# Image network with early fusion, one core: TensorE's four layers of a half batch written out instead of looped

## The reference

```python
x = coords @ fc0_w + fc0_b                 # 3 -> 32 channels
for sw, cw, cb in four_layers:
    x1 = _spectral_conv(x, sw)             # rfft2, a mix of 20 x 20 modes, irfft2
    x2 = einsum('bchw,oc->bohw', x, cw) + cb
    x = _gelu(x1 + x2)
x = _gelu(x @ fc1_w + fc1_b)
return (x @ fc2_w + fc2_b)[..., 0]
```

## Time and profile before

| | |
|---|---|
| median of 3 runs | 4595.69 us (4594.42 to 4607.03) |
| profiled execution, its own time | 4594.02 us |
| its span, first to last instruction | 4592.3 us |
| TensorE busy | 3972.5 us, 87% of the span |
| VectorE, ScalarE, GpSimd busy | 2471.1, 549.6, 651.3 us |
| mean granted clock of TensorE | 0.761 of full speed |

### The profile page before, as it was taken

The page is one execution under the profiler, slowest core; times in us unless marked ns, Lnnn a source line. Parts: engine busy times, 40 slices in busy tenths (PEclk is TensorE's granted clock), DMA queues, the critical chain, the costliest instruction groups (busy, mean ns, idle before and its releaser), DMA issues. The chain is left out here.

```text
span 4592.3 us, 117705 instructions
## 1 busy us (share of the span) xinstructions
PE 3972.5 (87%) x48492; PEld 3374.7 (73%) x48492; DVE 2471.1 (54%) x8074; ACT 549.6 (12%) x1173; POOL 651.3 (14%) x1708
## 2 busy tenths in 40 slices
PE   6999999999999999697657677898999989988687
PEld 5887888768888887454335576788998989986544
DVE  4444544244444452223656888787686775662422
ACT  0101011210010102211211110101000010001011
POOL 1000000000000000000002423232231231222121
PEclk9999999999999999787755555555555555556589
DMA  1000000000000000100003110101000000013111
GB/s 35 15 16 2 15 2 15 2 5 15 1 15 16 1 1 2 24 0 4 8 12 85 29 36 28 31 28 31 24 22 30 21 30 18 19 32 87 20 36 28
DMA packets 189733, 96.94 MB, mean 21 GB/s; under 512 B 139462, under 2 KB 172534, under 8 KB 188631
## 3 DMA queue, kind: packets, MB, share of 16 engines
q1 hardware_dynamic: 183574, 84.19, 7.8%
q10 hardware_dynamic: 4626, 7.39, 0.4%
q0 software_dynamic: 1280, 2.10, 0.2%
HBM read 76.11 MB, written 15.96 MB: 20 GB/s over the span
## 5 line engine op out<-in xcount | busy, mean ns | idle before, releaser
L1611 PE MATMUL sc_ps<-H,sc_cols 128*128 128x128 f32 x1536 | 393.8, 438 | 0.1
L1602 PE MATMUL sc_ps<-sc_h_now,sc_h_f 128*128 128x8 bf16 x11520 | 331.4, 168 | 40.2 <-DVE sc_h_now L1721 38.9
L340 PEld LDWEIGHTS im_acc<-im_cwt,im_chan 128*128 128x128 f32 x2048 | 268.7, 191 | 123.0 <-issue 123.0
L1602 PEld LDWEIGHTS sc_ps<-sc_h_now,sc_h_f 128*128 128x128 bf16 x11520 | 319.6, 104 | 45.3 <-DVE sc_h_now L1721 44.9
L1611 PEld LDWEIGHTS sc_ps<-H,sc_cols 128*128 128x128 f32 x1536 | 341.5, 327 | 0.7 <-POOL H L1502 0.2
L427 DVE COPY im_chan<-im_ring 128x512 f32<-128x512 f32 x256 | 173.6, 688 | 306.5 <-PE im_ring L296 306.5
L448 ACT ACTIVATE im_a<-im_acc 128x512 f32<-128x512 f32 x256 | 152.8, 597 | 1437.0 <-PE im_acc L340 1437.0
L338 PE MATMUL im_acc<-im_u,im_e 97*128 97x512 f32 x512 | 265.3, 599 | 37.5 <-DVE im_chan L427 37.5
L340 PE MATMUL im_acc<-im_cwt,im_chan 128*128 x2048 | 270.1, 274 | 0.0
L203 POOL DMA_DIRECT2D image_rows<-im_ho x16 | 9.5, 601 | 1821.0 <-DVEq L439 1821.0
L423 DVE COPY im_u<-im_ring 80x512 f32<-80x512 f32 x256 | 175.9, 687 | 145.1 <-PE im_ring L290 145.1
(11 more groups left out here) (387 smaller groups left out, 7003.4 us busy)
## 6 DMA issues: line engine op xcount, KB each, us to landing
sc_g_row<-mem_g_rows_dram SPq DMA_DIRECT2D x96, 256.0 KB, 3.5
im_wbd<-in_c_mix_dram SPq DMA_DIRECT2D x32, 400.0 KB, 5.9
sc_w_row<-mem_w_rows_dram SPq DMA_DIRECT2D x192, 64.0 KB, 2.5
sw_g_all<-sw_gates SPq DMA_DIRECT2D x8, 768.0 KB
mem_hist_h_dram<-sc_hist_h ACTq DMA_DIRECT2D x6, 512.0 KB, 3.6
mem_hist_dz_dram<-sc_hist_dz ACTq DMA_DIRECT2D x6, 512.0 KB, 4.6
mo_hist_dz<-mem_hist_dz_dram SPq DMA_DIRECT2D x8, 384.0 KB, 6.4
mo_hist_h<-mem_hist_h_dram SPq DMA_DIRECT2D x8, 384.0 KB, 6.6
```

The costliest lines, as they stand in the source:

```text
L340: mm = MM(acc[:, p % 2, m:512:4], chan[:, p % 2, m * 128:(m + 1) * 128], cwt[:, bass.ds(l, 1), :].rearrange("p a c -> p (a c)"), start=Fal ...
L1602: MM(score_h(g)[:, cc, b2 * QB:(b2 + 1) * QB], h_f[:, cc, w, a, (2 * b2 + g) * GW:(2 * b2 + g + 1) * GW], now(a, b2, m), start=n == 0, sto ...
L1611: mm = MM(hh(g), cols[:, b2, :], prod[:, g, a, b2 * GW:(b2 + 1) * GW], start=a + b2 == 0, stop=a + b2 == 2)
```

## The change

TensorE's loop over the four layers of a half becomes a Python loop, so that the layers are written out one behind the other in its instruction stream, twice four of them. With l a plain number, the counts that the waits compare with and the place of the channel weights are plain numbers too. The loops of VectorE (L386) and ScalarE (L444) stay.

```diff
@@ -304,7 +304,7 @@
                         pe.sem_inc(acc_read, 2)
                     input_layer(Fills(at), half)
                     at += FC0_FILLS
-                    with pe.Fori(0, NL) as l:
+                    for l in range(NL):
                         f = Fills(at, l * LAYER_FILLS)
                         first, acc_base = f.n, acc_at + l * LAYER_ACC
                         pe.wait_ge(acc_read, acc_base + 2)
```

## The result

The changed kernel takes 4583.8 us in the median of 15 runs (4569.8 to 4598.1), the kernel before, timed beside it, 4596.0 us (4588.1 to 4611.0). The ratio is 0.9969, 95% interval 0.9954 to 0.9984: faster, by about the 0.3% that can be told here. The median moved by 12.2 us where 18.5 were forecast, and lies in the range. The ratio stands for 14 us, and its interval for 7 to 21 us, so that the forecast lies inside it. The profiled execution is the shortest of the 15: 4569.8 us, 24.2 us under the profiled one of before.

The account below looks back on a forecast made before the run. TensorE was taken to bound the image network, the only stage changed. Terms 5.5 + 4.5 + 5.0 + 3.4 plus 0.1 gave 18.5 us, so 4595.7 - 18.5 = 4577.2 us, range 4568 to 4590 us.

Parts of the forecast that it names:

- Second stop: Matmuls stopping again for 1.83 us behind each of the first half's three branches at L307: 5.5 us go.
- First stop: First matmul stops behind six branches, 8.7 us together; 0.69 us each stays, waiting for ScalarE, so 4.5 us go.
- The wait's arithmetic: Register-computed wait counts delay matmuls at L276, L283 and L338; 0.62 us a layer, 5.0 us go (lower bound 1.4).
- The moved wait for the accumulator bank: Wait on L338's matmul becomes an instruction ahead: costs nothing; without cover up to 0.69 us at each of 256 positions.
- L257 at each half's start: Lag at the first layer of each half, counted as 0.13 us too: 0.1 us saved.
- The clock behind the double stop: Low-clock stretches of 3.4 us in the second and third layers, each losing 1.7 us, vanish: 3.4 us go.
- The fall after L290: Fourth layer's 13.7 us at 0.50 clock after L290's 1.42 us wait, costing 6.3 us; one such fall kept.
- the rival without a fall: No clock fall after L290 in the layers: 24.8 us saved, 4571 us; chance 0.24.
- the rival with one more: One more clock fall after L290 in the layers: 12.2 us saved, 4583 us; chance 0.20.
- The sum, 18.5 us: Saving over the layers: 5.5 + 4.5 + 5.0 + 3.4, plus 0.1 us; 14.8 with the register term's lower bound.
- straight code that can't be fetched fast enough: Up to 96 block boundaries in the layers stall 1.83 us each: 176 us slower, 4753 us; chance 0.05.
- stops that are covered anyway: TensorE's queued work covers the branch stops; only the register term, 5 us, remains: 4591 us; chance 0.06.

Follow-up runs that it names:

- the wait at L290 filled on both sides: Six unread matmuls per layer between L283 and L290: added to the changed kernel, 4570.9 us (ratio 0.9951); added to the kernel before, 4590.8 us (0.9991).
- the new order inside the layer: Changed kernel with each group's first transposes (L296) ahead of L290 and L338 waiting for L423's copies: 4529.9 us, ratio 0.9865.

## Why the prediction was right

- *Second stop, 5.5 us:* right. Straight code has none, and no wait inside a layer is put down to "issue".
- *First stop, 4.5 us:* right: 0.69 us at all six starts, which makes 4.6 of 8.7 - 6 x 0.69.
- *The wait's arithmetic, 5.0 us:* 5.2 measured. The lag became 0.06 us, as L362's was. With two layers a turn the registers alone gave 0.8 us a layer, of which 0.17 at its start, a part that the forecast has under the first stop.
- *The moved wait for the accumulator bank:* it cost nothing, as forecast. No wait at L338 is put down to ScalarE, and those for VectorE fell.
- *L257 at each half's start:* 0.83 us instead of 0.79; the lag there shrank by half of what was counted.
- *The clock behind the double stop, 3.4 us:* right. No layer of the changed kernel starts at low clock in three executions.
- *The fall after L290:* the price stood in the prediction (6.3 us in the kernel before, 5.9 in the changed one), the count couldn't. "I keep one such fall" treats it as the program's. It differs by execution: none, two and none in three profiles of one program, at equal waits. So the profiled execution came out at the time of the rival without a fall (4569.8 us, forecast 4571), and the median at that of the rival with one more (4583.8 us, forecast 4583). The latter is luck as far as the runs show: how many falls the other executions had isn't known, and times outside the layers vary too.
- *The sum, 18.5 us:* with the wait at L290 filled on both sides the change gives 18 to 20 us. With whatever falls each execution has, the medians give 12 and 17 us in two comparisons and the ratios 14 and 18. Both intervals hold 18.5, so that the shortfall of the first median isn't told from noise.
- *Not foreseen:* some 7 us between executions behind the image network, which the change doesn't touch. Where they come from stays open.
- *Two readings:* slices 2 to 16 of TensorE end at some 1,840 us and last 1,722. The median of 3.4 us for the branch at L307 counts the two that leave the loop; the six taken last 3.29 to 3.85 us. Neither enters the sum.
- *Rivals:* straight code that can't be fetched fast enough is out, as no wait inside a layer is put down to "issue"; stops that are covered anyway are out, as the layers became shorter by them.

## What to carry to other kernels

A loop can cost twice: by a stop of the queue at each branch back, here 3.29 us and more for a body of 1,400 matmuls and 0.2 us for the short loop at L1593 (the length at which the price changes wasn't measured), and, where a wait's count is computed, by a lag behind the waits, here 0.8 us a layer. Look at the branch's own duration, and at the lag between a producer's end and its consumer's start. The code behind the loop showed here already what is left when the loop is gone. When one program's executions differ by more than the change, compare profiles term by term, and look for clock that falls in some executions only; a forecast has to carry it as a spread. Ask last what the waits that are left are worth: the new order inside the layer gave more than the loop.

## What the runs showed of the hardware

- The branch back over a layer at L307 takes TensorE's queue 3.29 to 3.85 us, the one in the short loop at L1593 0.208 us in the median, and a branch not taken 0.07 to 0.08 us.
- Where a wait's count was computed in a register, the matmul started 0.13 or 0.23 us behind its producer; with a plain number L276 started 0.06 us behind it.
- What matmuls wait at such a branch differs in front of the same instructions: 1.2 to 1.6 us in one stop, 1.77 and 1.83 us, 1.20 and 2.28 us, or 4.27 us in one. Without a branch, 0.69 to 0.86 us of it is there too.
- After 1.42 us of idle, while L290's 80 x 80 products ran, the granted clock fell in some executions to 0.50 and stayed there for 13.7 us, past the end of the group's L290 and into the L283 behind it. With the wait filled it fell in none of the 16 layers of the two executions profiled.
